# Two-layer routed FFN: the first stage's product into the ranks with the high and low halves of A in one weight

## The chip, the cores and the metric

The kernel runs on one core of one Trainium2 chip. The metric is the device time of one execution in microseconds. Before the change three runs took 981.65, 980.63 and 980.98 us: the median is 980.98 us.

## What is computed

Two layers work on x, 128 sequences of 32 tokens with 512 features (4096 tokens). Cut to the part that the change touches, with the rest in a line each:

```python
def _L0_cond_ref(x, adapter_mapping, W, b, lora_As, lora_Bs):   # W 512x512, As 32x512x16, Bs 32x16x512
    base_out = jnp.einsum('bti,oi->bto', x, W) + b
    A = lora_As[adapter_mapping]                # one adapter of 16 ranks for each sequence b
    Bm = lora_Bs[adapter_mapping]
    lora_h = jnp.einsum('bti,bir->btr', x, A)   # the product into the ranks
    lora_out = jnp.einsum('btr,bro->bto', lora_h, Bm)
    return base_out + lora_out * SCALING        # SCALING = 2

x = x + _L0_ffn_ref(_L0_cond_ref(x, itok_B_0_23, ...), ...)   # gate, up, silu, down; 1376 wide
x = x + _L1_ffn_ref(_L1_cond_ref(x, itok_B_0_7, ...), ...)    # routed, 8 experts of 16 ranks each
```

## The kernel before, in words

Features lie on the 128 partitions in KC = 4 chunks, tokens on the free axis, in NT = 8 tiles of TOK = 512 tokens. Float32 products are made of fp32r parts: ScalarE writes a rounded high part (`..._hi`), VectorE the rest (`..._lo`), and `mm3` (in `pe_program`) issues three matmuls, high weight x high, high weight x low and low weight x high. The low x low product is left out.

The work has three stages in order. The first makes c = `_L0_cond_ref(x)` of all tiles, in the first 142 us of the span. The second is the FFN of layer 0 in the form of a Strassen-like scheme over four pairs of tiles, up to about 805 us. The third folds layer 1's weights together and applies them with its routers. Only the first stage is changed; the others come after it on TensorE.

In the first stage a tile of 512 tokens holds 16 sequences, which form NG = 2 groups of GB = 8. The adapters of the 8 sequences of a group, 16 ranks each, make 128 columns. SyncE (for group 1 of tile 0: GpSimd) gathers them by `gather_a` into `a_raw`, one DMA a sequence; GpSimd gathers the rows of B into `b_raw`. `turn_a` in `act_program` (L1049) splits them into `a_hi` and `b_hi`, and its namesake in `dve_program` (L1510) makes `a_lo` and `b_lo`. `lora_in` in `pe_program` (L1978) is **the product into the ranks**: for each group and chunk, `mm3` with the 128 rank columns of all 8 sequences as the weight and the group's 256 tokens streaming. Each token thus gets the ranks of 8 sequences, of which only its own is wanted. `lora_in` in `dve_program` (L1521) masks the bank with `own_batch`, which is 1 where partition and token belong to the same sequence, and scales it by 2 into `h_masked`. ScalarE's `lora_in` (L1066) makes `lh_hi` of it, VectorE then `lh_lo`, and `lora_out` on TensorE (L2214) multiplies by B into the four banks of c. `close_c` on ScalarE (L1072) moves these to `c_out`, and GpSimd stores them to HBM. The weight that a matmul uses is loaded by an instruction of its own ahead of it (PEld in the profile).

The order on TensorE is written out by hand at the end of `pe_program`. Tiles 0 and 1 share their base product: after three of four chunks comes `lora_in(0)`, then the rest of the base, `lora_out(0)`, `lora_in(1)`, one more block of base matmuls (12 of 512 columns), `lora_out(1)`. From tile 2 on a tile is two base blocks of 12 (`cond_base`), `lora_in(t)`, two more blocks, `lora_out(t)`. ScalarE does for each tile `turn_a(t)`, the split of x for the next tile, `lora_in(t)`, then `close_c` mixed with splits of later weights (`down_hi`); VectorE the same on its side. From tile 6 on both also prepare the second stage: `cop_split` and `cop_begin`, `cop_rest` read the first c back from HBM (`load_c` on SyncE), and in tile 7 `gate_up_hi` and `gate_up_lo` split seven weights ahead of `lora_in`.

Semaphores tie the parts together: `a_lo_done` lets TensorE start a group, `pe_ring` says that the bank of ranks is full, `dve_freed` that VectorE has read it, `lh_lo_done` that `lora_out` may start.

Of the kernel before, what the change touches and what calls it, by code (L numbers as in the profile page):

```python
# [6 lines left out]
ALU = mybir.AluOpType  # L7
# [21 lines left out]
def build(nc, x, slots, slot_list, langs, w0, b0, a_cols, b_rows, w_gate, w_up, w_down, wb1, rhs2, ra1, b2t, b1, out):  # L29
# [65 lines left out]
    a_hi = work("a_hi", [NG, KC, P], F32R)  # L95
    a_lo = work("a_lo", [NG, KC, P], F32R)
# [37 lines left out]
    warm = work("warm", [TOK], F32R)  # L134

# [190 lines left out]
    a_hi_done, a_lo_done = sem("a_hi_done"), sem("a_lo_done")  # L326
    b_hi_done, b_lo_done = sem("b_hi_done"), sem("b_lo_done")
# [64 lines left out]
    ZEROS, ROWS = 1, 4  # L392
# [131 lines left out]
    def a_views(g, half):  # L524
        return (half[:, g, :, :].rearrange("p k (b r) -> p k b r", b=GB),
                a_raw[:, g, :, :].rearrange("p b (k r) -> p k b r", k=KC))
# [51 lines left out]
    def sync_program(e):  # L578
# [11 lines left out]
        def gather_a(t, gs=range(NG)):  # L590

            for g in gs:
                if t > 0:
                    e.wait_ge(a_lo_done, NG * (t - 1) + g + 1)
                for b in range(GB):
                    slot = e.snap(slot_regs[g * GB + b], min_val=0, max_val=a_cols.shape[0] - 1)  # L596
                    e.dma_start(a_raw[:, g, b, :], a_cols[bass.ds(slot, 1)].rearrange("s p c -> (s p) c")).then_inc(  # L597
                        a_in[g], DMA)
# [253 lines left out]
    def pool_program(e):  # L852
# [107 lines left out]
        for b in range(GB):  # L960
            slot = e.snap(slot_regs[b], min_val=0, max_val=a_cols.shape[0] - 1)
            e.dma_start(a_raw[:, 1, b, :], a_cols[bass.ds(slot, 1)].rearrange("s p c -> (s p) c")).then_inc(a_first_in, DMA)
# [74 lines left out]
    def act_program(e):  # L1037
# [11 lines left out]
        def turn_a(t):  # L1049
            for g in range(NG):  # L1050
# [7 lines left out]
                a_to, a_from = a_views(g, a_hi)  # L1058
                e.activation(a_to, a_from, ACT.Copy).then_inc(a_hi_done, 1)
            for g in range(NG):  # L1060
# [3 lines left out]
                e.activation(b_hi[t % 2][:, g, :], b_raw[g][:, :], ACT.Copy).then_inc(b_hi_done, 1)  # L1064

        def lora_in(t):  # L1066
            e.wait_ge(dve_freed, ring_freed("h", t, 0)[1])
# [424 lines left out]
    def dve_program(e):  # L1492
# [17 lines left out]
        def turn_a(t):  # L1510
            for g in range(NG):
                e.wait_ge(a_hi_done, NG * t + g + 1)
                a_to, a_from = a_views(g, a_lo)
                a_high, _ = a_views(g, a_hi)
                e.tensor_tensor(a_to, a_from, plain(a_high), ALU.subtract).then_inc(a_lo_done, 1)
            for g in range(NG):
                e.wait_ge(b_hi_done, NG * t + g + 1)
# [3 lines left out]
        def lora_in(t):  # L1521
# [4 lines left out]
            else:  # L1526
                e.wait_ge(lh_lo_done, t)
            e.scalar_tensor_tensor(
                out=h_masked[:, :].rearrange("p (g c) -> p g c", g=NG),
                in0=ring_bank("h", t, 0)[:, :].rearrange("p (g c) -> p g c", g=NG), scalar=SCALING,  # L1530
# [251 lines left out]
        assert links[0] == ZEROS  # L1782
        e.wait_ge(pool_const, 1)
# [591 lines left out]
```

## Time and profile before

| | |
|---|---|
| median of 3 runs | 980.98 us (980.63 to 981.65) |
| profiled execution, its own time | 981.22 us |
| its span, first to last instruction | 979.5 us |
| TensorE matmuls, busy | 972.1 us, 4723 |
| weight loads (PEld), busy | 822.1 us, 4723 |
| VectorE, ScalarE, GpSimd busy | 586.0, 464.5, 276.9 us |
| mean granted TensorE clock | 1.000 |

Times in the rows are in microseconds unless marked ns; ACT is ScalarE, DVE VectorE, POOL GpSimd, SP SyncE, PE TensorE. A row of a timeline holds the start, the time from the first start to the last end of the instructions merged in it, the engine, the line in the code, the operation, out<-in with its shape, and how many (x). In brackets stands how long the engine idled before, and what released it. Matmuls overlap, so the distance of two starts is less than the duration that a row shows.

### The profile page before, as it was taken

Reading aid. Unit: us, or ns where it says so; the run is one execution under the profiler, and the core shown is the slowest. Engines: PE = TensorE matmul, PEld = TensorE weight load, DVE = VectorE, ACT = ScalarE, POOL = GpSimd, SP = SyncE. Lnnn points to the kernel's source line nnn. Section 1 sums busy time; section 2 is a strip of 40 time slices with the busy share of each in tenths; the row PEclk is TensorE's granted clock in tenths of the full one; section 3 lists DMA queues with packets and bytes.
Section 4 is the critical chain, followed back from the end, with each engine's and each line's share of the span. In section 5 each row is a group of like instructions: output and inputs, shape, how many; then the busy total and the mean of one; then the engine's idle time right before and its main releaser. Section 6 shows DMA issues by size and latency. Waiting matters only on the chain.

```text
span 979.5 us, 14271 instructions
## 1 busy us (share of the span) xinstructions
PE 972.1 (99%) x4723; PEld 822.1 (84%) x4723; DVE 586.0 (60%) x970; ACT 464.5 (47%) x855; POOL 276.9 (28%) x284
## 2 busy tenths in 40 slices
PE   9999999999999999999999999999999999999998
PEld 7888888888888888888888888888888899898986
DVE  4545487876992432685423398333278488786862
ACT  4646476655742333571333383233357264545342
POOL 5363524654300721400522230261140460000000
PEclk9999999999999999999999999999999999999999
DMA  7899868686968866877886777987688650616132
GB/s 239 269 362 321 265 232 300 243 295 243 369 237 296 295 195 193 278 235 263 278 278 195 234 246 249 322 280 194 194 275 314 236 194 22 236 37 223 65 108 86
DMA packets 131123, 230.14 MB, mean 235 GB/s; under 512 B 29798, under 2 KB 29799, under 8 KB 130539
## 3 DMA queue, kind: packets, MB, share of 16 engines
q1 hardware_dynamic: 126720, 216.35, 66.4%
q0 software_dynamic: 4192, 12.87, 3.6%
q8 instruction: 39, 0.64, 0.3%
q14 instruction: 34, 0.27, 0.1%
q10 hardware_dynamic: 138, 0.01, 0.0%
HBM read 165.74 MB, written 63.44 MB: 234 GB/s over the span
## 4 chain that ended last, share of the span: by engine, by line
PE 87%; SPq 5%; DVE 2%; DMA 2%; issue 2%; ACT 1%; ACTq 0%; DVEq 0%
PE bank L1951 87%; SPq L597 3%; DMA x_raw<-in_x 1%; PE bank L2114 1%; SPq L583 1%; DMA c<-c_scratch 1%; SPq L588 0%; DMA a_raw<-in_a_cols 0%; SPq L664 0%; DVE xa_lo L1502 0%; ACT c_out L1076 0%; SPq L596 0%; ACT dt L1102 0%; SPq L772 0%; DVE hg L1762 0%
## 5 line engine op out<-in xcount | busy, mean ns | idle before, releaser
L1951 PE MATMUL bank<-cop_hi,wring 128*128 128x512 f32 x1234 | 380.9, 389 | 0.0
L1951 PEld LDWEIGHTS bank<-cop_hi,wring 128*128 128x128 f32 x1234 | 231.6, 188 | 48.8 <-DVE v L1590 0.4
L1951 PE MATMUL bank<-cop_lo,wring 128*128 128x512 f32 x616 | 239.7, 389 | 0.0
L1951 PE MATMUL bank<-op_hi,wring 128*128 128x512 f32 x560 | 173.8, 389 | 0.0
L1590 DVE TENSOR_TENSOR v<-bank,p7s 128x512 f32<-128x512 f32 x44 | 30.4, 691 | 194.0 <-PE bank L1951 193.9
L1951 PEld LDWEIGHTS bank<-cop_lo,wring 128*128 128x128 f32 x616 | 115.6, 188 | 24.0
L1951 PEld LDWEIGHTS bank<-op_hi,wring 128*128 128x128 f32 x560 | 105.1, 188 | 22.0 <-DMA wring<-wd_scratch 0.2
L1951 PE MATMUL bank<-op_lo,wring 128*128 128x512 f32 x280 | 108.9, 389 | 0.0
L1176 ACT ACTIVATE s<-bank 128x512 f32<-128x512 f32 x44 | 26.3, 597 | 112.6 <-PE bank L1951 112.6
L1576 DVE TENSOR_TENSOR op_lo<-h,op_hi 128x512 fp32r<-128x512 f32 x100 | 72.6, 743 | 3.7 <-ACT op_hi L1133 3.6
L909 POOL TENSOR_TENSOR h_t<-h,h 128x512 f32<-128x512 f32 x20 | 27.1, 1356 | 160.8 <-DVE h L1612 160.8
L1133 ACT ACTIVATE op_hi<-h 128x512 fp32r<-128x512 f32 x100 | 62.6, 626 | 13.9 <-PE bank L1951 12.8
L1145 ACT ACTIVATE bank<-bank 128x512 f32<-128x512 f32 x44 | 25.6, 583 | 76.5 <-PE bank L1951 76.5
L1951 PEld LDWEIGHTS bank<-op_lo,wring 128*128 128x128 f32 x280 | 52.6, 188 | 10.9
L948 POOL TENSOR_TENSOR t_sum<-x_second,x_second 128x256 f32<-128x256 f32 x12 | 9.4, 817 | 177.6 <-DMA x_second<-x_scratch 177.6
L1951 PE MATMUL bank<-xa_hi,w_hi 128*128 128x512 f32 x128 | 46.9, 392 | 1.2 <-ACT w_hi L1047 0.8
L1951 PE MATMUL bank<-xa_lo,w_hi 128*128 128x512 f32 x128 | 46.7, 390 | 0.0
L1951 PE MATMUL bank<-xa_hi,w_lo 128*128 128x512 f32 x128 | 46.5, 389 | 0.0
L1595 DVE TENSOR_TENSOR p7s<-bank,p7s 128x512 f32<-128x512 f32 x44 | 30.4, 691 | 24.9 <-PE bank L1951 24.9
L1167 ACT ACTIVATE s<-bank 128x512 f32<-128x512 f32 x44 | 26.3, 598 | 30.6 <-PE bank L1951 30.6
L1152 ACT ACTIVATE p7s<-bank 128x512 f32<-128x512 f32 x44 | 26.3, 598 | 30.2 <-PE bank L1951 30.1
L1160 ACT ACTIVATE bank<-bank 128x512 f32<-128x512 f32 x44 | 25.6, 582 | 30.0 <-PE bank L1951 30.0
(243 smaller groups left out, 1925.8 us busy)
## 6 DMA issues: line engine op xcount, KB each, us to landing
wring<-wgu_scratch SPq DMA_DIRECT2D x231, 256.0 KB, 3.1
wring<-wd_scratch SPq DMA_DIRECT2D x140, 256.0 KB, 5.5
wgu_scratch<-wring SPq DMA_DIRECT2D x77, 256.0 KB, 3.5
c_scratch<-c_out POOLq DMA_DIRECT2D x32, 256.0 KB, 3.3
c<-c_scratch SPq DMA_DIRECT2D x32, 256.0 KB, 4.7
xs_raw<-x_scratch SPq DMA_DIRECT2D x16, 512.0 KB, 5.2
out<-res SPq DMA_DIRECT2D x32, 256.0 KB, 2.1
x_raw<-in_x SPq DMA_DIRECT2D x14, 512.0 KB, 5.8
```

What stands on the lines that cost most here:

```text
L597: e.dma_start(a_raw[:, g, b, :], a_cols[bass.ds(slot, 1)].rearrange("s p c -> (s p) c")).then_inc(a_in[g], DMA)
L909: e.tensor_tensor(h_t3[p][:, :], h22[p][:, :], h12[p][:, :], ALU.subtract).then_inc(t3_done, 1)
L1133: e.activation(op_hi[n % N_OP][:, :], op_source[i][p][:, :], ACT.Copy).then_inc(op_hi_done, 1)
L1145: e.activation(bank_y[b][:, :], bank_a[b][:, :], ACT.Copy).then_inc(ay_done, 1)
L1152: e.activation(p7s[b][:, :], bank_w[b][:, :], ACT.Copy).then_inc(p7s_done, 1)
L1160: e.activation(bank_z[b][:, :], bank_y[b][:, :], ACT.Copy).then_inc(yz_done, 1)
L1167: e.activation(s1[j % 2][:, :], bank_a[j % 2][:, :], ACT.Silu).then_inc(silu1_done, 1)
L1176: e.activation(s2[j % 2][:, :], bank_z[j % 2][:, :], ACT.Silu).then_inc(silu2_done, 1)
L1576: e.tensor_tensor(op_lo[n % N_OP][:, :], op_source[i][p][:, :], plain(op_hi[n % N_OP][:, :]), ALU.subtract).then_inc(op_lo_done, 1)
L1590: e.tensor_tensor(v[b][:, :], bank_z[b][:, :], p7s[b][:, :], ALU.add).then_inc(gc22_done, 1)
L1595: e.tensor_tensor(p7s[b][:, :], bank_y[b][:, :], p7s[b][:, :], ALU.add).then_inc(gc21_done, 1)
L1951: return e.matmul(out_ap, lhs, rhs, start=start, stop=stop, skip_group_check=True)
```

## The change

In place of `a_hi` and `a_lo` there is one tile `a_both` with 256 columns for each group and chunk: low parts of four sequences (64 columns), high parts of all eight (128), low parts of the other four (64). Columns 0 to 127 are low and high of one half of the sequences, columns 128 to 255 high and low of the other half. `gather_a` puts the sequences into `a_raw` in the order that this takes (`a_place`). TensorE goes over each group twice, 128 tokens at a time, with the weight of the four sequences to which these tokens belong, and streams the high and the low part of x past it: two matmuls a chunk in place of three. The bank then holds the product with the high columns in one half of the partitions and with the low columns in the other; of the low ones also the part from the low x, which the kernel before left out. To add the halves, ScalarE copies each to the other half of the partitions (`lora_turn`, two operations, into `h_turned`), VectorE adds bank and `h_turned` into `h_masked`, and masks and scales that as before. VectorE makes the low columns in two operations a group. `h_turned` is cleared once at the start, so that its unused quarters are finite. The semaphores `a_hi_done` and `b_hi_done` become one.

```diff
--- before.py
+++ after.py
@@ -92,8 +92,7 @@
     within(h_region + 4 * ROW, h10_region - h_region - 4 * ROW)
     a_raw = work("a_raw", [NG, GB, KC * R], F32)
     b_raw = [work(f"b_raw{g}", [D], F32) for g in range(NG)]
-    a_hi = work("a_hi", [NG, KC, P], F32R)
-    a_lo = work("a_lo", [NG, KC, P], F32R)
+    a_both = work("a_both", [NG, KC, 2 * P], F32R)
     w0_hi = work("w0_hi", [KC, D], F32R)
     w0_lo = work("w0_lo", [KC, D], F32R)
     b_hi = [work(f"b_hi{s}", [NG, D], F32R) for s in range(2)]
@@ -132,6 +131,7 @@
 
     within(w_region, N_W * ROW)
     warm = work("warm", [TOK], F32R)
+    h_turned = sb("h_turned", [NG, GT], F32, w_region + 8 * ROW)
 
     gs_first = [sb(f"gs_first{i}", [2, P], F32, w_region + (N_W - 2) * ROW + (i - 1) * ROW // 2) for i in range(1, 5)]
 
@@ -323,8 +323,8 @@
     x_hi, x_lo = sem("x_hi"), sem("x_lo")
     l_hi, l_lo = sem("l_hi"), sem("l_lo")
     w0_hi_done, w0_lo_done = sem("w0_hi_done"), sem("w0_lo_done")
-    a_hi_done, a_lo_done = sem("a_hi_done"), sem("a_lo_done")
-    b_hi_done, b_lo_done = sem("b_hi_done"), sem("b_lo_done")
+    ab_hi_done, a_lo_done, b_lo_done = sem("ab_hi_done"), sem("a_lo_done"), sem("b_lo_done")
+    h_turned_done = sem("h_turned_done")
     lh_hi_done, lh_lo_done = sem("lh_hi_done"), sem("lh_lo_done")
     c_closed, l_closed = sem("c_closed"), sem("l_closed")
     act_freed, dve_freed = sem("act_freed"), sem("dve_freed")
@@ -389,7 +389,7 @@
 
     IDENT, MASK, LATER, EXPERT = 3, 6, 8, 9
 
-    ZEROS, ROWS = 1, 4
+    ZEROS, ROWS = 1, 5
 
     def x_parts(t):
 
@@ -521,9 +521,22 @@
 
 
 
-    def a_views(g, half):
-        return (half[:, g, :, :].rearrange("p k (b r) -> p k b r", b=GB),
-                a_raw[:, g, :, :].rearrange("p b (k r) -> p k b r", k=KC))
+    HB, HR = GB // 2, P // 2
+
+    def a_views(g, b, at_col):
+        n = b.stop - b.start
+        return (a_both[:, g, :, at_col:at_col + n * R].rearrange("p k (b r) -> p k b r", b=n),
+                a_raw[:, g, b, :].rearrange("p b (k r) -> p k b r", k=KC))
+
+    def a_place(b):
+
+        return (b + HB) % GB
+
+    def h_turns():
+
+        for rows, other, tok in ((slice(0, HR), slice(HR, P), slice(0, GT // 2)),
+                                 (slice(HR, P), slice(0, HR), slice(GT // 2, GT))):
+            yield rows, other, tok
 
     def g_sums(j):
         return gs_first if j == 0 else gs[j % 2]
@@ -594,7 +607,7 @@
                     e.wait_ge(a_lo_done, NG * (t - 1) + g + 1)
                 for b in range(GB):
                     slot = e.snap(slot_regs[g * GB + b], min_val=0, max_val=a_cols.shape[0] - 1)
-                    e.dma_start(a_raw[:, g, b, :], a_cols[bass.ds(slot, 1)].rearrange("s p c -> (s p) c")).then_inc(
+                    e.dma_start(a_raw[:, g, a_place(b), :], a_cols[bass.ds(slot, 1)].rearrange("s p c -> (s p) c")).then_inc(
                         a_in[g], DMA)
 
         def load_gate_up(j):
@@ -959,7 +972,7 @@
         e.reg_load(slot_regs, slot_sb[0:1, GB:2 * GB])
         for b in range(GB):
             slot = e.snap(slot_regs[b], min_val=0, max_val=a_cols.shape[0] - 1)
-            e.dma_start(a_raw[:, 1, b, :], a_cols[bass.ds(slot, 1)].rearrange("s p c -> (s p) c")).then_inc(a_first_in, DMA)
+            e.dma_start(a_raw[:, 1, a_place(b), :], a_cols[bass.ds(slot, 1)].rearrange("s p c -> (s p) c")).then_inc(a_first_in, DMA)
         gather(0)
         e.memset(own_batch[:, :], 1.0).then_inc(pool_const, 1)
         mask_view = own_batch[:, :].rearrange("p (b t) -> p b t", b=GB)
@@ -1055,15 +1068,27 @@
                     e.wait_ge(a_in[g], GB * DMA * (t + 1 - g))
                 if t > 0:
                     e.wait_ge(pe_ring, ring_full("h", t - 1, 0))
-                a_to, a_from = a_views(g, a_hi)
-                e.activation(a_to, a_from, ACT.Copy).then_inc(a_hi_done, 1)
+                a_to, a_from = a_views(g, slice(0, GB), HR)
+                e.activation(a_to, a_from, ACT.Copy).then_inc(ab_hi_done, 1)
             for g in range(NG):
                 e.wait_ge(b_in, NG * DMA * (t + 1))
                 if t > 1:
                     e.wait_ge(pe_acc, nth(t - 2))
-                e.activation(b_hi[t % 2][:, g, :], b_raw[g][:, :], ACT.Copy).then_inc(b_hi_done, 1)
+                e.activation(b_hi[t % 2][:, g, :], b_raw[g][:, :], ACT.Copy).then_inc(ab_hi_done, 1)
+
+        def lora_turn(t):
+            both = ring_bank("h", t, 0)[:, :].rearrange("p (g c) -> p g c", g=NG)
+            e.wait_ge(pe_ring, ring_full("h", t, 0))
+            if t == 0:
+                e.wait_ge(dve_chain, ZEROS + 1)
+            else:
+                e.wait_ge(dve_freed, ring_freed("h", t - 1, 0)[1])
+            for rows, other, tok in h_turns():
+                done = e.activation(h_turned[rows, :, tok], both[other, :, tok], ACT.Copy)
+            done.then_inc(h_turned_done, 1)
 
         def lora_in(t):
+            lora_turn(t)
             e.wait_ge(dve_freed, ring_freed("h", t, 0)[1])
             if t > 1:
                 e.wait_ge(pe_acc, nth(t - 2))
@@ -1509,12 +1534,14 @@
 
         def turn_a(t):
             for g in range(NG):
-                e.wait_ge(a_hi_done, NG * t + g + 1)
-                a_to, a_from = a_views(g, a_lo)
-                a_high, _ = a_views(g, a_hi)
-                e.tensor_tensor(a_to, a_from, plain(a_high), ALU.subtract).then_inc(a_lo_done, 1)
+                e.wait_ge(ab_hi_done, 2 * NG * t + g + 1)
+                for b, at_col, hi_col in ((slice(0, HB), 0, HR), (slice(HB, GB), P + HR, P)):
+                    a_to, a_from = a_views(g, b, at_col)
+                    a_high, _ = a_views(g, b, hi_col)
+                    done = e.tensor_tensor(a_to, a_from, plain(a_high), ALU.subtract)
+                done.then_inc(a_lo_done, 1)
             for g in range(NG):
-                e.wait_ge(b_hi_done, NG * t + g + 1)
+                e.wait_ge(ab_hi_done, 2 * NG * t + NG + g + 1)
                 e.tensor_tensor(b_lo[t % 2][:, g, :], b_raw[g][:, :], plain(b_hi[t % 2][:, g, :]),
                                 ALU.subtract).then_inc(b_lo_done, 1)
 
@@ -1525,9 +1552,13 @@
                 e.wait_ge(w0_lo_done, KC)
             else:
                 e.wait_ge(lh_lo_done, t)
+            both = ring_bank("h", t, 0)[:, :].rearrange("p (g c) -> p g c", g=NG)
+            whole = h_masked[:, :].rearrange("p (g c) -> p g c", g=NG)
+            e.wait_ge(h_turned_done, t + 1)
+            linked(e.tensor_tensor(whole, both, h_turned[:, :, :], ALU.add))
+            e.wait_ge(dve_chain, links[0])
             e.scalar_tensor_tensor(
-                out=h_masked[:, :].rearrange("p (g c) -> p g c", g=NG),
-                in0=ring_bank("h", t, 0)[:, :].rearrange("p (g c) -> p g c", g=NG), scalar=SCALING,
+                out=whole, in0=whole, scalar=SCALING,
                 in1=own_batch[:, :].unsqueeze(1).to_broadcast([P, NG, GT]),
                 op0=ALU.mult, op1=ALU.mult).then_inc(dve_freed, 1)
             e.wait_ge(lh_hi_done, t + 1)
@@ -1780,6 +1811,7 @@
 
         linked(e.memset(plain(warm[:, :]), 0.0))
         assert links[0] == ZEROS
+        linked(e.memset(h_turned[:, :, :], 0.0))
         e.wait_ge(pool_const, 1)
         linked(e.tensor_single_scalar(r_i[:, :], part_i[:, :], R - 1, ALU.bitwise_and))
         e.wait_ge(dve_chain, links[0])
@@ -1980,12 +2012,15 @@
             bank = take_h(t)
             for g in range(NG):
                 e.wait_ge(a_lo_done, NG * t + g + 1)
-                for k in range(KC):
-                    if g == 0:
-                        e.wait_ge(x_lo, x_n(t, k))
-                    tok = slice(g * GT, (g + 1) * GT)
-                    done = mm3(bank[:, tok], a_hi[:, g, k, :], a_lo[:, g, k, :],
-                               xa_hi[s][:, k, tok], xa_lo[s][:, k, tok], k == 0, k == KC - 1)
+                for first in (P, 0):
+                    at_tok = g * GT + (0 if first == P else GT // 2)
+                    tok = slice(at_tok, at_tok + GT // 2)
+                    for k in range(KC):
+                        if (g, first) == (0, P):
+                            e.wait_ge(x_lo, x_n(t, k))
+                        both = a_both[:, g, k, first:first + P]
+                        mm(bank[:, tok], both, xa_hi[s][:, k, tok], k == 0, False)
+                        done = mm(bank[:, tok], both, xa_lo[s][:, k, tok], False, k == KC - 1)
             done.then_inc(pe_ring, 1)
 
         def cond_base(t, m, k):
```

The order of instructions on TensorE, in the first tile's product into the ranks (`xa` is x, the number behind a name its buffer, x3 and x4 how many like it follow one another). Before:

```order
L1951 MATMUL bank<-xa_lo_72,w_hi 128x512 x3
L1951 MATMUL bank<-xa_hi_70,w_lo 128x512 x3
L1951 MATMUL bank<-xa_hi_69,a_hi 128x256
L1951 MATMUL bank<-xa_lo_71,a_hi 128x256
L1951 MATMUL bank<-xa_hi_69,a_lo 128x256
```

and with the change:

```order
L1983 MATMUL bank<-xa_lo_71,w_hi 128x512 x3
L1983 MATMUL bank<-xa_hi_69,w_lo 128x512 x3
L1983 MATMUL bank<-xa_hi_68,a_both 128x128
L1983 MATMUL bank<-xa_lo_70,a_both 128x128
L1983 MATMUL bank<-xa_hi_68,a_both 128x128
```

The three rows of 256 columns come eight times before, the two of 128 columns sixteen times with the change; what stands ahead and behind is unmoved.

The order on ScalarE in tile 2, before:

```order
L1064 ACTIVATE b_hi_61<-b_raw_55 128x512
L1064 ACTIVATE b_hi_61<-b_raw_56 128x512
L1043 ACTIVATE xa_hi_70<-x_raw_75 128x512 x4
L1070 ACTIVATE lh_hi_65<-h_masked 128x512
L1076 ACTIVATE c_out_51<-bank,b_287 128x512
```

and with the change:

```order
L1077 ACTIVATE b_hi_60<-b_raw_55 128x512
L1077 ACTIVATE b_hi_60<-b_raw_56 128x512
L1056 ACTIVATE xa_hi_69<-x_raw_74 128x512 x4
L1087 ACTIVATE h_turned<-bank 64x2x128 x2
L1095 ACTIVATE lh_hi_64<-h_masked 128x512
L1101 ACTIVATE c_out_51<-bank,b_287 128x512
```

The two copies stand between the split of x and `lh_hi`. On VectorE one addition stands ahead of the mask.

## Rows read from the trace of the kernel before

**Rows 1.** The page: TensorE's busy time, its granted clock in 40 slices, the chain

```profile
PE 972.1 (99%) x4723; PEld 822.1 (84%) x4723; DVE 586.0 (60%) x970; ACT 464.5 (47%) x855; POOL 276.9 (28%) x284
...
PEclk9999999999999999999999999999999999999999
...
PE 87%; SPq 5%; DVE 2%; DMA 2%; issue 2%; ACT 1%; ACTq 0%; DVEq 0%
```

**Rows 2.** Waits from 0 to 140 us: total, times, longest

```profile
PE bank L1951 <- DVE lh_lo L1534: 0.9, 1, 0.9
...
PE bank L1951 <- ACT c_out L1076: 0.4, 1, 0.4
```

**Rows 3.** Timeline of TensorE, first tile's product into the ranks and what follows

```profile
20.52 0.28 PE L1951 MATMUL bank<-xa_hi,a_hi 128*128 128x256 f32 x1
...
23.39 1.09 PE L1951 MATMUL bank<-xa_hi,w_hi 128*128 128x512 f32 x4
```

**Rows 4.** Timeline of loads (PEld), then of matmuls, behind tile 1's wait

```profile
37.73 0.19 PEld L1951 LDWEIGHTS bank<-lh_hi,b_hi 128*128 128x128 f32 x1 [1.32 <-DVE lh_lo L1534]
37.84 0.19 PEld L1951 LDWEIGHTS bank<-lh_lo,b_hi 128*128 128x128 f32 x1
37.96 0.19 PEld L1951 LDWEIGHTS bank<-lh_hi,b_lo 128*128 128x128 f32 x1
...
37.74 0.39 PE L1951 MATMUL bank<-lh_hi,b_hi 128*128 128x256 f32 x1 [0.90 <-DVE lh_lo L1534]
37.96 0.28 PE L1951 MATMUL bank<-lh_lo,b_hi 128*128 128x256 f32 x1
```

**Rows 5.** Timeline of TensorE's shortest matmuls, then of the loads behind them

```profile
846.50 1.09 PE L1951 MATMUL bank<-ra,hg1t 128*128 128x136 f32 x8
847.43 0.60 PE L2114 MATMUL bank<-ident,hg 128*128 128x128 f32 x4
...
847.75 0.19 PEld L1951 LDWEIGHTS bank<-hg_hi,m_hi 128*128 128x128 f32 x1
847.87 0.19 PEld L1951 LDWEIGHTS bank<-hg_lo,m_hi 128*128 128x128 f32 x1
```

**Rows 6.** 256 elements on ScalarE and VectorE (timelines); the page on a 512 add

```profile
129.18 0.72 ACT L1089 ACTIVATE wring<-gs_first 128x256 fp32r<-128x256 f32 x2
...
130.49 0.75 DVE L1540 TENSOR_TENSOR wring<-gs_first,wring 128x256 fp32r<-128x256 f32 x2
...
L1590 DVE TENSOR_TENSOR v<-bank,p7s 128x512 f32<-128x512 f32 x44 | 30.4, 691 | 194.0 <-PE bank L1951 193.9
```

**Rows 7.** Timelines of TensorE and VectorE in tile 3, from the product's end

```profile
65.73 0.40 PE L1951 MATMUL bank<-xa_hi,w_hi 128*128 128x512 f32 x1
...
71.20 0.28 PE L1951 MATMUL bank<-lh_hi,b_hi 128*128 128x256 f32 x1
...
66.63 0.68 DVE L1528 SCALAR_TENSOR_TENSOR h_masked<-bank,own_batch 128x512 f32<-128x512 f32 x1
68.01 0.84 DVE L1534 TENSOR_TENSOR lh_lo<-h_masked,lh_hi 128x512 fp32r<-128x512 f32 x1 [0.70 <-ACT lh_hi L1070]
```

**Rows 8.** Timelines of TensorE and VectorE in tile 1, from the product's end

```profile
33.81 0.28 PE L1951 MATMUL bank<-xa_hi,a_lo 128*128 128x256 f32 x1
33.93 0.40 PE L1951 MATMUL bank<-xa_hi,w_hi 128*128 128x512 f32 x1
...
35.62 0.67 DVE L1528 SCALAR_TENSOR_TENSOR h_masked<-bank,own_batch 128x512 f32<-128x512 f32 x1
36.99 0.69 DVE L1534 TENSOR_TENSOR lh_lo<-h_masked,lh_hi 128x512 fp32r<-128x512 f32 x1 [0.70 <-ACT lh_hi L1070]
```

**Rows 9.** Timelines of TensorE and ScalarE between tiles 6 and 7

```profile
123.99 0.28 PE L1951 MATMUL bank<-lh_hi,b_lo 128*128 128x256 f32 x1
124.71 0.50 PE L1951 MATMUL bank<-xa_hi,w_hi 128*128 128x512 f32 x1 [0.43 <-ACT c_out L1076]
...
120.50 0.63 ACT L1115 ACTIVATE cop_hi<-c 128x512 fp32r<-128x512 f32 x1 [0.20 <-DMA c<-c_scratch]
```

**Rows 10.** Timeline of VectorE in tile 7

```profile
135.18 0.69 DVE L1554 TENSOR_TENSOR c_t<-c,c 128x512 f32<-128x512 f32 x1 [2.60 <-DMA c<-c_scratch]
...
137.89 0.69 DVE L1534 TENSOR_TENSOR lh_lo<-h_masked,lh_hi 128x512 fp32r<-128x512 f32 x1 [0.70 <-ACT lh_hi L1070]
```

## The prediction

> **What bounds the kernel now.** I read the page first: TensorE is busy 99% of the span and holds 87% of the chain that ended last [rows 1]. So I took the waits of the first 140 us, where the changed stage lies: TensorE idles 0.9 us for `lh_lo` and 0.4 us for `c_out`, and nothing else there holds it up [rows 2]. The time is therefore the sum of what TensorE issues, one start after the other. A matmul's duration says little, since they overlap; what counts is the distance between starts, and that I take from TensorE's timeline.
>
> In the first tile's product into the ranks, 24 matmuls of 256 columns fill 20.52 to 23.39, where the next work starts: 2.87 us, 0.120 each [rows 3]. 24 matmuls of 512 columns fill 65.73 to 71.20: 0.228 each [rows 7]. The difference of 0.108 us is 256 columns at 2.4 GHz, the level that a granted clock of 1.00 is. So a matmul of n columns costs n/2.4 ns and some 13 ns, as long as its columns are what it waits for.
>
> **The change, part by part.**
>
> *Streamed columns.* A tile's product goes from 24 matmuls of 256 columns to 32 of 128, from 6144 to 4096 columns. By columns alone one of 128 would cost 53 + 13 = 67 ns and a tile 32 x 0.067 = 2.14 us in place of 2.87.
>
> *Weight loads.* But each matmul has its own load of 128 x 128 weights: as many of the one as of the other [rows 1, 3]. What a load costs when nothing covers it is seen after a wait: TensorE starts one at 37.73 and the next at 37.84. The matmul that is noted at 37.74 has 0.39 us where its like have 0.28, so it really ran 0.11 us later, when its load was through [rows 4]. In a stream, each load starts with the matmul ahead of it (both at 37.96): one load is under way per matmul, not two. So two starts cannot be closer than one load, about 0.108 us with 0.003 for the hand-over. The shortest distances in the trace agree: 8 matmuls of 136 columns fill 846.50 to 847.43, 0.116 us each, and 4 transposes of 128 columns last 0.60 us with 0.27 for the last, 0.11 us each [rows 5]. Both are plain fp32 and might be slow for another reason. But the loads at 847.75 and 847.87 are again a whole load apart, and the first is of the kernel's own kind. Under 256 columns (107 ns) a load was covered; under 128 it isn't. Bounds for the unseen case: 67 ns, and 0.111 + 0.013 = 0.124 us if the 13 ns come on top of the load. I take 0.111 us, which these measured loads are nearest to [rows 4, 5]: 32 x 0.111 = 3.55 us, **0.68 us more a tile, 5.4 us for eight**.
>
> The Trainium skill ("TensorE: Matmul & The Clock Gate", Back-to-back issue gap) has a measured sustained rate of about 81 ns for a load and a matmul of 128 columns. By that a tile would take 2.59 us and eight would save 2.2 us. The trace has no distance that short.
>
> *The way back to TensorE.* ScalarE now first turns two quarters of the bank: two operations of 256 elements, and a pair of these took 0.72 us [rows 6]. VectorE then adds (0.69, as an add out of a bank [rows 6]) before the old mask. From the mask's start to TensorE's next use it was 35.62 to 37.74, 2.12 us, the last hand-over in it 0.06 (37.68 to 37.74) [rows 4, 8]. With three more such hand-overs: 0.06 + 0.72 + 0.06 + 0.69 + 0.06 + 2.12 = 3.7 us from the product's end, 1.5 us more than before. The cover in tiles 2 to 7 is the 24 base matmuls behind the product, 5.5 us. In tile 3, the tightest of 2 to 6, `lh_lo` ended at 68.86, 2.3 us early [rows 7]. There the mask began at 66.63, 0.7 us behind the product's end, since VectorE was busy; the turning covers that. Left over: 5.5 + 0.1 - 0.3 - 3.7 = 1.6 us (a last matmul runs some 0.3 us past its start, and the next starts 0.1 behind it). So it costs nothing; without the cover it would be 1.5 us a tile. Tile 0 has 21 base matmuls, 4.8 us, and 0.9 us left.
>
> *Tile 1* has only 12, from 33.93 [rows 8]. They ended at 36.67, and TensorE waited until 37.74. The mask began 1.5 us behind the product's end, VectorE being held by tile 2's x, whose arrival does not hang on TensorE. Two longer products put TensorE 1.4 us later, which takes this part away, and the wait is again 0.3 + 3.7 - 2.85 = 1.1 us. Before: 1.1. Nothing; at worst 1.5 us, if x moves along with TensorE.
>
> *Tile 6 to 7.* At 124.71 TensorE starts 0.6 us late: ScalarE came late to `c_out`, since it had to split loaded c first, which came by DMA as late as 120.50 [rows 9]. TensorE will be 7 x 0.68 = 4.8 us later by then; the DMA less, since it hangs on earlier tiles. I count -0.6 us, with 0 for the bound.
>
> *Tile 7.* The mask was late here, behind sums of c that waited 2.60 us for DMA, and `lh_lo` ended at 138.58, just at its use [rows 10]. The turning is over by then; the add costs 0.7 us if the DMA moves with TensorE in full. With TensorE 5.4 us later I expect slack instead: 0, bound +0.7.
>
> *Small ones.* The low part of A in two pieces of 256 costs VectorE 2 x 0.34 us (0.75 less the last 0.41 [rows 6]), some 0.1 more than one of 512; TensorE needs the second group 1.4 us behind the first. `h_turned` is cleared once at the start, while VectorE waits for x. ScalarE is held at the turn, but its next job, `c_out`, waits for TensorE anyway.
>
> **Sum.** 5.4 - 0.6 = +4.8 us on the profiled execution's 981.22 gives 986.0; the median shown is 0.24 lower, so **985.8 us**.
>
> **Rivals.**
> 1. *Loads are hidden, columns decide.* If a load could start ahead of the matmul before it, or two neighbours with the same weights shared one, a tile costs 2.14 us: 8 x -0.73 = -5.8, 975 us, faster. It decides from a distance under 0.090 us, where 32 matmuls cost what 24 did. For it: 16 of 32 weights are repeats. Against: the loads measured [rows 4, 5], among them `b_hi` loaded twice in a row. 7%. By the 81 ns of the skill it is 978.8 us; 3%.
> 2. *The 13 ns come on top of the load.* 0.124 us, +1.10 a tile, 8.8 - 0.6, 989 us. In the range.
> 3. *The hand-over becomes a wait.* If ScalarE or VectorE comes to the turn so late that `lh_lo` misses its use by 1 us in each of tiles 2 to 6, +5 us on top, 991 us. For it: two more crossings between engines. Against: the 1.6 us left. 8%.
> 4. *The clock.* A stream that holds columns half of the time could let the granted clock fall to 1.2 GHz. It stayed 1.00 in every slice, waits and transposes included [rows 1]. If the 12 matmuls behind each product ran at that level, 0.43 us in place of 0.23, it would be +2.4 us a tile, 1005 us. 4%.
> 5. *The columns are not fewer.* The order of instructions shows 32 of 128 columns, so no.
>
> **Numbers.** A measurement of this kernel tells 0.2% (2 us) from no change. The forecast with its bounds has 74%; its range is 983.5 (0.102 us, a little under the shortest distance seen) to 990 (0.124 us, both small terms at their bad ends). A distance near 0.09 us, so no change, has 4%. With rival 3 the range to 991.5 holds 82%. Faster 10%, same 4%, slower 86%.
>
> **What would show it.** In the timeline after: loads and matmuls of the product 0.11 us apart; a product of 3.5 us; `lh_hi` some 1.4 us later behind it; no wait for `lh` in tiles 2 to 7, 1.1 us in tile 1, none near tile 6's `c_out`; the clock at 1.00; from 145 us on everything as before, only later. A product of 2.1 us would make me wrong in sign.

## The result and the profile after

The changed kernel took 986.75 us, the median of 4 runs (986.12 to 987.73), beside 981.32 us (980.63 to 982.16) for the kernel before: a ratio of 1.0054, 95% interval 1.0040 to 1.0068. Five more runs on another chip gave 985.95 beside 981.35 us, 1.0058 (1.0045 to 1.0071). The forecast was 985.8 us, range 983.5 to 991.5. The profiled execution took 986.12 us, with a span of 984.5 us; before it was 979.5.

The page of the changed kernel, the lines that answer to [rows 1]:

```profile
PE 978.0 (99%) x4787; PEld 828.4 (84%) x4787; DVE 592.2 (60%) x995; ACT 470.3 (48%) x871; POOL 282.1 (29%) x284
...
PEclk9999999999999999999999999999999999999999
...
PE 97%; DVE 2%; ACT 1%; DMA 0%; issue 0%; DVEq 0%; ACTq 0%
```

There are 64 matmuls more (8 tiles, 32 in place of 24), the clock is at its higher level throughout, and TensorE holds still more of the chain. What TensorE waited for from 0 to 145 us (total, times, longest), as in [rows 2]:

```profile
PE bank L1983 <- DVE warm L1812: 1.7, 1, 1.7
PE bank L1983 <- DVE lh_lo L1565: 1.0, 1, 1.0
```

The wait for `c_out` is gone; `warm` is from the start-up, before the changed stage's first product. The first tile's product in TensorE's timeline, which answers to [rows 3], and below it the loads:

```profile
20.85 0.22 PE L1983 MATMUL bank<-xa_hi,a_both 128*128 128x128 f32 x1
20.91 0.28 PE L1983 MATMUL bank<-xa_lo,a_both 128*128 128x128 f32 x1
21.02 0.27 PE L1983 MATMUL bank<-xa_hi,a_both 128*128 128x128 f32 x1
...
24.37 1.16 PE L1983 MATMUL bank<-xa_hi,w_hi 128*128 128x512 f32 x4
...
20.96 0.19 PEld L1983 LDWEIGHTS bank<-xa_hi,a_both 128*128 128x128 f32 x1
21.07 0.19 PEld L1983 LDWEIGHTS bank<-xa_lo,a_both 128*128 128x128 f32 x1
```

Matmuls and loads alike start 0.11 us apart, and 32 matmuls fill 20.85 to 24.37: 3.52 us, where 24 took 2.87. The first step is only 0.06 us, and that comes back when the stream ends: the second 512-column matmul behind the product starts 0.29 us after the first, where before it was 0.24. From the product's first matmul to that second one it is 3.81 us in all eight tiles, and 3.11 before: **+0.70 us a tile, 5.6 us in all**.

The way back in tile 3 (ScalarE, VectorE, TensorE), which answers to [rows 7]:

```profile
69.18 0.77 ACT L1087 ACTIVATE h_turned<-bank 64x256 f32<-64x256 f32 x2 [2.49 <-PE bank L1983]
...
70.08 0.69 DVE L1558 TENSOR_TENSOR h_masked<-bank,h_turned 128x512 f32<-128x512 f32 x1 [1.87 <-ACT h_turned L1087]
...
70.81 1.47 DVE L1560 SCALAR_TENSOR_TENSOR h_masked<-h_masked,own_batch 128x512 f32<-128x512 f32 x1
...
72.98 1.00 DVE L1565 TENSOR_TENSOR lh_lo<-h_masked,lh_hi 128x512 fp32r<-128x512 f32 x1 [0.70 <-ACT lh_hi L1095]
...
74.53 0.28 PE L1983 MATMUL bank<-lh_hi,b_hi 128*128 128x256 f32 x1
```

The turning took 0.77 us (forecast 0.72) and the add 0.69, as forecast. The mask took 1.47 us here and `lh_lo` 1.00, where either took 0.69 in tiles 4 to 7 (in tile 2 it was 1.08 and 1.00); `lh_lo` still ended 0.55 us ahead of its use. That slack was 0.96 us in tile 0, 0.95 in tile 2, 1.64 in tiles 4 to 6 and 1.47 in tile 7. Tile 1, from the product's end (TensorE, ScalarE, VectorE), answers to [rows 8]:

```profile
35.64 0.44 PE L1983 MATMUL bank<-xa_hi,w_hi 128*128 128x512 f32 x1
...
39.61 0.39 PE L1983 MATMUL bank<-lh_hi,b_hi 128*128 128x256 f32 x1 [0.99 <-DVE lh_lo L1565]
...
35.84 0.77 ACT L1087 ACTIVATE h_turned<-bank 64x256 f32<-64x256 f32 x2 [0.67 <-PE bank L1983]
...
36.74 0.69 DVE L1558 TENSOR_TENSOR h_masked<-bank,h_turned 128x512 f32<-128x512 f32 x1 [0.74 <-ACT h_turned L1087]
...
38.86 0.69 DVE L1565 TENSOR_TENSOR lh_lo<-h_masked,lh_hi 128x512 fp32r<-128x512 f32 x1 [0.70 <-ACT lh_hi L1095]
```

Tiles 6 to 7 on TensorE [rows 9], then tile 7 on VectorE [rows 10] and TensorE's use of `lh_lo`:

```profile
129.52 0.28 PE L1983 MATMUL bank<-lh_hi,b_lo 128*128 128x256 f32 x1
129.64 0.40 PE L1983 MATMUL bank<-xa_hi,w_hi 128*128 128x512 f32 x1
...
138.58 0.69 DVE L1585 TENSOR_TENSOR c_t<-c,c 128x512 f32<-128x512 f32 x1 [1.42 <-DMA c<-c_scratch]
...
142.02 0.69 DVE L1565 TENSOR_TENSOR lh_lo<-h_masked,lh_hi 128x512 fp32r<-128x512 f32 x1 [0.70 <-ACT lh_hi L1095]
...
144.19 0.28 PE L1983 MATMUL bank<-lh_hi,b_hi 128*128 128x256 f32 x1
```

**The account.** The second stage starts at 147.06 us, 5.45 later than before (141.61). Tile 0's product began 0.33 us later, from the start-up. The products cost 5.6 us. In tile 1 the two starts around the wait are 1.375 us apart and were 1.288: +0.1. The late start in tile 7 (0.71 us where 0.12 is usual) is gone: -0.6. These make 5.4. Three starts of 0.34 to 0.39 us in place of 0.23 in the second stage's first 10 us (at 141.9, 150.2 and 150.5 before) are gone too, 0.4 us given back, and the span is 5.0 us longer.

### The profile page after: what moved, and what is told of

It reads as the page before. It is cut to its first block, busy times and chain, and to the rows that moved or that the text cites. A ratio compares the mean times of both kernels' runs of the same rounds, so it can differ in the third digit from the quotient of the medians.

```text
span 984.5 us, 14449 instructions
## 1 busy us (share of the span) xinstructions
PE 978.0 (99%) x4787; PEld 828.4 (84%) x4787; DVE 592.2 (60%) x995; ACT 470.3 (48%) x871; POOL 282.1 (29%) x284
## 4 chain that ended last, share of the span: by engine, by line
PE 97%; DVE 2%; ACT 1%; DMA 0%; issue 0%; DVEq 0%; ACTq 0%
PE bank L1983 96%; PE bank L2149 1%; DMA x_raw<-in_x 0%; DVE t_lo L1684 0%; DVE hg L1793 0%; DVE greater L1773 0%; ACT t_hi L1260 0%; DVE lx L1809 0%; DVE wins L1769 0%; DVE rank L1776 0%; DVE greater L1767 0%; ACT h_turned L1087 0%; DVE res L1701 0%; DVE h_masked L1560 0%; DVE lh_lo L1565 0%
```

## The experiments

**What sets the distance.** Three kernels change one size of the product's matmuls each, and keep 32 of them a tile. `half_columns` streams 64 tokens in each, so it leaves out the ranks of half of the tokens:

```diff
+                        tok_ = slice(at_tok, at_tok + GT // 4)
-                        mm(bank[:, tok], both, xa_hi[s][:, k, tok], k == 0, False)
+                        mm(bank[:, tok_], both, xa_hi[s][:, k, tok_], k == 0, False)
```

(and `xa_lo` alike).

> The changed kernel with each of the 32 matmuls of a tile's product into the ranks streaming 64 columns in place of 128, so half of the tokens get no ranks; the loads are as they were. If the distance of two starts is one weight load, nothing moves: 0.111 us each, a product of 3.5 us, 986.5 us or so. If it is set by the columns (128 / 2.4 ns and a fixed part of 58 ns), it falls to 0.084 us, 0.85 us less a tile, 980 us.

TensorE in the first tile's product:

```profile
20.87 0.28 PE L1983 MATMUL bank<-xa_hi,a_both 128*128 128x64 f32 x1
20.98 0.28 PE L1983 MATMUL bank<-xa_lo,a_both 128*128 128x64 f32 x1
```

Half the columns, and still 0.11 us: the columns don't set it. The profiled execution took 985.53 us with a span of 983.9. The median of 4 is 988.02 us, ratio 1.008 (1.0052 to 1.0107), because two executions took 990.5 and 992.7 us with a mean granted clock of 0.994 and 0.993; the other two took 985.5 us. Those with the lower clock were not profiled, so what brought it down stays open. `half_weights` keeps 128 tokens and loads 64 weight columns; it leaves out the half of the result that the other 64 give:

```diff
-                        both = a_both[:, g, k, first:first + P]
-                        mm(bank[:, tok], both, xa_hi[s][:, k, tok], k == 0, False)
+                        both = a_both[:, g, k, first:first + P // 2]
+                        mm(bank[0:P // 2, tok], both, xa_hi[s][:, k, tok], k == 0, False)
```

> The changed kernel with only the first 64 of the 128 weight columns in each matmul of the product (64 partitions of the bank get a result), all else the same, 128 tokens streaming. If the load sets the distance and costs by its columns, it falls to what 128 streamed columns need, 0.067 us: 32 x 0.044 = 1.4 us less a tile, 11.3 us in all, 975.5 us. If the load is a fixed time, or the distance is a floor for issuing a load and a matmul, it stays at 0.111 us and 986.5 us.

```profile
21.25 0.22 PE L1983 MATMUL bank<-xa_hi,a_both 128*64 128x128 f32 x1
21.31 0.22 PE L1983 MATMUL bank<-xa_lo,a_both 128*64 128x128 f32 x1
```

With the load halved the same 128 columns stream every 0.060 us. So the distance is not a fixed price for issuing a load and a matmul: **it is the load's**. `half_weights` also halves the partitions that a matmul writes, but the load's own record shrinks with it, from 0.192 to 0.135 us, by 0.057 us where the distance shrinks by 0.051. But the kernel took 982.04 us (10 runs, ratio 1.0000, 0.9987 to 1.0012) and not 12.9 us less than the change (8 x 1.61). In tile 1 TensorE now stood for `lh_lo`:

```profile
39.30 0.58 PE L1983 MATMUL bank<-lh_hi,b_hi 128*128 128x256 f32 x1 [3.35 <-DVE lh_lo L1565]
39.68 0.41 PE L1983 MATMUL bank<-lh_lo,b_hi 128*128 128x256 f32 x1
...
30.49 0.63 ACT L1072 ACTIVATE a_both<-a_raw 128x512 fp32r<-128x512 f32 x1 [3.07 <-DMA a_raw<-in_a_cols]
...
32.06 2.41 ACT L1101 ACTIVATE c_out<-bank,b 128x512 f32<-128x512 f32 x4
...
35.54 0.77 ACT L1087 ACTIVATE h_turned<-bank 64x256 f32<-64x256 f32 x2
```

The start distance there is 3.73 us in place of 1.38, since ScalarE's queue up to the turn (`b_hi`, `c_out`, `xa_hi`) hangs on the gather of A, for which ScalarE waited until 30.49 us. Behind this wait the clock fell: the matmul at 39.68 shows 0.41 us where its like have 0.28, its followers start 0.21 us apart, and the use of `lh` took 5.29 us in place of 2.97. Further waits stand at 99.3, 125.6 and 139.1 us (start distances of 0.62, 1.27 and 0.69): TensorE's saved time went into waits for other engines and into the lower clock. `wide_columns` streams all 256 tokens of the group in each of the 32, so half of the ranks are those of the wrong sequences:

```diff
+                    tok = slice(g * GT, (g + 1) * GT)
```

> The changed kernel with each of the 32 matmuls streaming all 256 tokens of its group, twice the columns; the second pass overwrites the first, so half of the ranks are those of the wrong sequences. Load theory: 256 columns just cover a load, so the distance is the 0.120 us seen before: +0.3 us a tile, +2.3 us in all, 989 us, though the columns double. Column theory (a fixed 58 ns on top of the columns): 0.165 us, +1.7 us a tile, 1000 us.

```profile
22.89 0.28 PE L1983 MATMUL bank<-xa_hi,a_both 128*128 128x256 f32 x1
23.00 0.28 PE L1983 MATMUL bank<-xa_lo,a_both 128*128 128x256 f32 x1
```

Twice the columns cost 0.26 us a tile (4.07 for 3.81). The time was 988.26 us (4 runs, ratio 1.0065, 1.0050 to 1.0079); its profiled execution also began the first product 2 us late. In a table, with the median distance of two starts in the product (the last column takes 0.111 us for a load of 128 weight columns, and half of it for 64):

| weight columns x tokens | distance, us | by columns (n/2.4 + 13 ns) | by the load |
|---|---|---|---|
| 128 x 64 | 0.112 | 0.040 | 0.111 |
| 128 x 128 | 0.111 | 0.067 | 0.111 |
| 128 x 256 | 0.120 | 0.120 | 0.111 |
| 64 x 128 | 0.060 | 0.067 | 0.056 |

The larger of the two columns fits the three rows with a full weight. At 64 x 128 the two nearly meet, and the measured 60 ns lies between them, so the 13 ns are not a fixed price either.

**The two halves of the change, each alone.** `chain_alone` keeps the turning and the add but issues the product as before (with the wrong columns of A for the low part). `product_alone` is the reverse: 32 matmuls of 128 columns, without turning and add, so the low half of the product is left out. The matmuls of `chain_alone`:

```diff
+                    done = mm3(bank[:, tok], a_both[:, g, k, P // 2:P // 2 + P], a_both[:, g, k, 0:P],
+                               xa_hi[s][:, k, tok], xa_lo[s][:, k, tok], k == 0, k == KC - 1)
```

and, of `product_alone`, the lines without turning and add:

```diff
-            lora_turn(t)
-            linked(e.tensor_tensor(whole, both, h_turned[:, :, :], ALU.add))
-                out=whole, in0=whole, scalar=SCALING,
+                out=whole, in0=both, scalar=SCALING,
```

> The changed kernel with TensorE's product as before, 24 matmuls of 256 columns (the wrong columns of A for the low part, so the result is not the reference's); the turning by ScalarE, the extra add and the split low part of A stay. My theory: the way back is hidden, so this is the kernel before within 1 us (981 to 982 us), with the waits in tile 1 0.9 to 1.5 us longer than before at worst. Rival: the longer way back is what the change costs, then it shows most of the 5.4 us, 985 us or more.

> The changed kernel with its 32 matmuls of 128 columns but without the turning and the add: the mask reads the bank, and the low half of the product is lost. My theory: all of the cost stays but what tile 1's wait gives, 985 to 986.5 us. Rival (the way back costs): it falls to the kernel before, 981 us.

`chain_alone` took 983.13 us (12 runs) beside 981.47, 1.0015 (1.0007 to 1.0024). So the way back alone, without the longer product, costs 1.7 us, more than the 1 us expected. The profiled execution was the slowest of the twelve (984.9 us). Its tile 1 on TensorE, ScalarE's wait for the gather ahead of it, and one window (busy times, granted clock, DMA share, GB/s):

```profile
39.64 0.39 PE L1983 MATMUL bank<-lh_hi,b_hi 128*128 128x256 f32 x1 [2.48 <-DVE lh_lo L1565]
...
40.87 0.41 PE L1983 MATMUL bank<-lh_hi,b_hi 128*128 128x256 f32 x1
41.08 0.41 PE L1983 MATMUL bank<-lh_lo,b_hi 128*128 128x256 f32 x1
...
30.84 0.63 ACT L1072 ACTIVATE a_both<-a_raw 128x512 fp32r<-128x512 f32 x1 [3.27 <-DMA a_raw<-in_a_cols]
...
40.00:60.00 20.00, 20.00 (x114) 18.07 (x113) 10.45 (x18) 11.02 (x21) 12.87 (x11) 0.91 1.00 352
```

The two starts around the wait are 2.87 us apart, 1.58 more than in the trace of the kernel before, and 1 us behind it the clock fell. In tiles 3 and 7 `lh_lo` ended just at its use as well (start distances 0.46 and 0.37 us). But the longer chain is not all of the 1.58 us. The mask started 1.88 us later than before (37.50 for 35.62), and 1.00 of that is the gather of A, for which ScalarE waited until 30.84 us here and until 29.84 in the trace of the kernel before; 0.88 is the turning and the add, and TensorE itself came 0.32 us later. This gather moves without any change to the first tiles. In `before_order` below, where everything up to tile 6 is the kernel before (the rows of before, then those of `before_order`):

```profile
29.84 0.63 ACT L1059 ACTIVATE a_hi<-a_raw 128x512 fp32r<-128x512 f32 x1 [2.90 <-DMA a_raw<-in_a_cols]
...
31.16 0.63 ACT L1059 ACTIVATE a_hi<-a_raw 128x512 fp32r<-128x512 f32 x1 [3.22 <-DMA a_raw<-in_a_cols]
...
39.05 0.39 PE L1952 MATMUL bank<-lh_hi,b_hi 128*128 128x256 f32 x1 [1.88 <-DVE lh_lo L1534]
```

The mask starts 5.8 us behind `a_hi` in both, since `b_hi`, `c_out`, `xa_hi` and VectorE's `xa_lo` stand between. With the gather 1.3 us later the start distance is 2.27 us in place of 1.29, and the clock fell behind it. `before_light` (31.04 us, 2.32 us) shows the same. **So the one trace of the kernel before, on which the forecast rests, had one of the shorter waits in tile 1.** The changed kernel doesn't feel the gather there: in both its traces ScalarE stood waiting for the product when it came to the turn (0.67 us in the first), and the distance was 1.38 and 1.37 us.

`product_alone` took 984.84 us (6 runs), 1.0030 (1.0018 to 1.0042). To set it beside the whole change on one chip, both ran again:

> The changed kernel once more, beside its own part product_alone (32 matmuls of 128 columns, no turning and no add) and the kernel before. If the longer way from the product back to TensorE is covered, as forecast, this run equals product_again within 0.5 us and both stand some 5 us over the kernel before. The earlier runs, on separate chips, had 986.75 us here and 984.84 us for product_alone, against 981.3 and 981.5 us of the kernel before: so the rival says that 1 to 2 us of the change belong to the way back.

> As product_alone: leaves out the turning and the add, so each token lacks part of its ranks' sum. Way back covered: the same as after_again, 986 to 987 us. Way back not covered: 1 to 2 us under after_again, 985 us.

985.95 us (5 runs, 985.67 to 988.02) for the change, and 984.98 us (5 runs, 984.40 to 985.43; 1.0044, 1.0031 to 1.0057) without the way back: 1.0 us apart where at most 0.5 was expected, so in the changed kernel the way back is not free. In the second trace of `product_alone` the place is plain: the mask starts as soon as the product ends, and TensorE runs on into `lh_hi` (TensorE, then VectorE):

```profile
37.90 0.39 PE L1979 MATMUL bank<-xa_hi,w_lo 128*128 128x512 f32 x1
38.12 0.28 PE L1979 MATMUL bank<-lh_hi,b_hi 128*128 128x256 f32 x1
...
35.51 0.69 DVE L1556 SCALAR_TENSOR_TENSOR h_masked<-bank,own_batch 128x512 f32<-128x512 f32 x1
36.90 0.69 DVE L1561 TENSOR_TENSOR lh_lo<-h_masked,lh_hi 128x512 fp32r<-128x512 f32 x1 [0.70 <-ACT lh_hi L1094]
```

No wait in tile 1 here, with the gather of A in use at 29.58 us; in the first trace, where it was 31.29, the distance was 0.96 us from start to start.

**Can the halves in one weight be had without short matmuls?** `two_banks` joins the high and the low x of 128 tokens into one matmul of 256 columns, from tile 2 on: 16 matmuls a tile into two banks, and two adds more on VectorE. It computes what the changed kernel does.

```diff
+                            done = mm(h_banks(t)[g][:, q * GT:(q + 1) * GT].rearrange("p (n c) -> p n c", n=2),
+                                      a_both[:, g, k, first:first + P], xa_parts[:, :, s, k, tok],
+                                      k == 0, k == KC - 1)
...
+                    linked(e.tensor_tensor(to, part[:, :, 0, :], other, ALU.add))
+                    linked(e.tensor_tensor(to, part[:, :, 1, :], to, ALU.add))
```

> The same result with half of the loads: from tile 2 on a matmul streams the high and the low part of x of its 128 tokens, 256 columns in all, past one load, into separate columns of two banks; ScalarE turns a group's quarters while TensorE still works on the other group, and VectorE adds in two steps a group. Load theory: 16 x 0.120 = 1.92 us for a product in place of 3.52, six tiles: -9.6 us from the changed kernel, 977 us, 4 us under the kernel before. If the column count alone set the time, the 4096 columns are the same and it stays at 986.5 us. If the longer way through ScalarE and VectorE misses the next use in some tiles, up to 1 us each comes back.

A product took 2.15 us, 1.66 less than in the change and 0.96 less than before. Yet the time was 982.47 us (12 runs, 1.0007, 0.9999 to 1.0016). In tile 5 TensorE stood for the low part of A (TensorE, ScalarE, windows):

```profile
96.17 1.11 PE L2012 MATMUL bank<-xa_parts,a_both 128*128 128x256 f32 x8
99.36 1.22 PE L2012 MATMUL bank<-xa_parts,a_both 128*128 128x256 f32 x8 [2.08 <-DVE a_both L1559]
...
97.89 0.63 ACT L1078 ACTIVATE a_both<-a_raw 128x512 fp32r<-128x512 f32 x1 [4.64 <-DMA a_raw<-in_a_cols]
...
80.00:100.00 20.00, 17.92 (x103) 15.46 (x102) 11.16 (x23) 11.03 (x24) 4.92 (x6) 1.00 1.00 335
100.00:120.00 20.00, 20.00 (x103) 17.28 (x103) 13.06 (x26) 11.37 (x25) 13.15 (x16) 0.91 0.90 286
```

The gather landed late at a DMA share of 1.00, and the clock fell behind the wait. `lh_lo` was late too, in tile 2 (start distance 1.00 us, behind a mask of 2.41 us) and in tile 7 (1.63 us), so here the way back cost time as well. To stay out of the late gather, `mixed` leaves tiles 0 to 3 as before and takes the two banks from tile 4 on (`SPLIT = 4`). It also masks ahead of the first sums of c in tile 7, a move that `before_order` makes alone:

```diff
+            lora_in(t)
+            if t == NT - 1:
                 cop_begin(0, 1)
-            lora_in(t)
```

> The kernel before with one move on VectorE: in tile 7 the mask and the low part of the ranks' result stand ahead of the first sums of c, which wait 2.60 us for DMA. In the kernel before that low part ended 0.08 us behind its use, so TensorE lost next to nothing there. If tile 7 costs nothing: within 0.5 us of the kernel before. If the sums of c, now later, hold up the second stage's start: 0.5 to 1.5 us slower. It is the control for mixed, which has this move too.

> The product as in the kernel before in tiles 0 to 3, and in tiles 4 to 7 as in two_banks: 16 matmuls of 256 columns, the high and the low part of x in one matmul and two banks. No load is uncovered at 256 columns, and the late tiles leave the gather of A more time. From the lengths measured before, 2.15 us in place of 2.87 us of the kernel before in 4 tiles: -2.9 us, and the wait of 1 us in tile 1 stays as it is. Load theory, with all waits covered: 978.5 us. If the gather of A (DMA share 0.94 to 1.00 in this stretch) or the way back takes the gain again, as in two_banks: 980.5 to 982 us.

`before_order` took 980.86 us (12 runs, 0.9999, 0.9989 to 1.0009): no difference. `mixed` took 980.97 us (11 runs, 1.0001, 0.9992 to 1.0011), which undoes the change's loss but gains nothing. The wait in tile 5 had come back, and behind it one for `lh_lo` (start distance 1.01 us). TensorE, ScalarE, window:

```profile
99.04 1.22 PE L2013 MATMUL bank<-xa_parts,a_both 128*128 128x256 f32 x8 [2.31 <-DVE a_both L1562]
...
97.56 0.63 ACT L1079 ACTIVATE a_both<-a_raw 128x512 fp32r<-128x512 f32 x1 [4.87 <-DMA a_raw<-in_a_cols]
...
80.00:100.00 20.00, 17.69 (x104) 15.42 (x104) 10.93 (x21) 10.81 (x23) 5.04 (x7) 1.00 1.00 333
```

The last gather of that group was issued at 91.3 us, and ScalarE waited until 97.56 for it; in the kernel before it was issued at 91.8 and had landed at 94.9. The last pair asks whether the DMA's load does this. In both kernels SyncE's stores of W_down's sums, and their later reads, take 16 of 128 partitions, so most of the down product is left out:

```diff
+            few = P // 8
-            e.dma_start(wd_dram[g, i][:, 0:c, :],
+            e.dma_start(wd_dram[g, i][0:few, 0:c, :],
```

> before_order with less to move: of the sums of W_down that SyncE stores to scratch ahead of each gather of A (14 stores of 512 KB from 20 to 140 us), only 16 of 128 partitions are stored and later read back, so the output is without most of the down product. TensorE's instructions stay the same. This is the baseline of mixed_light. In before TensorE waits 0.9 us for the ranks of tile 1 and 0.4 us for c_out and nothing for the gather, so both theories expect before_order's time less at most 1.5 us: 979.5 to 981 us.

> mixed with the same lighter stores; the output is without most of the down product. mixed had four products of 2.15 us in place of 3.11 us, 3.8 us in all, but its time was the kernel before's: TensorE stood 2.6 us in tile 5 for the low part of A, whose last gather had landed shortly before, at a DMA share of 1.00, and 1.0 us for lh_lo. If the DMA's load took the gain: no wait at tile 5 here, and 3 to 4 us under before_light, some 976.5 us. If the gather's own chain (one small DMA after another, released by VectorE's low part) or the engines' order took it, whatever else is moved: the wait at tile 5 stays at 1 to 2.6 us and the time is within 1.5 us of before_light.

`before_light` took 981.08 us (11 runs, 0.9998, 0.9989 to 1.0007), `mixed_light` 977.51 us (8 runs, 0.9968, 0.9957 to 0.9978): 3.6 us less, where four products of 0.96 us less make 3.8. Tile 5 of `mixed_light` (TensorE, window):

```profile
95.59 2.08 PE L2015 MATMUL bank<-xa_parts,a_both 128*128 128x256 f32 x16
...
80.00:100.00 20.00, 20.00 (x116) 17.65 (x115) 14.80 (x29) 12.05 (x27) 9.40 (x8) 1.00 0.82 236
```

No wait, and a DMA share of 0.82. A shorter product is thus worth its full length, and what took it back was the DMA's load. The lightened stores stand ahead of the gathers of A on SyncE's queue, so the pair does not tell whether the gathers gained by less traffic or by less in front of them. The kernel before had a share of 0.96 in the same stretch, so it had little room.

## Why the prediction was right, point by point

- *What bounds.* TensorE's issue, start after start: right. 5.0 us of span are 5.6 of product and small terms.
- *Weight loads, 0.111 us each, 5.4 us.* Right: 0.110 measured as a mean, 5.6 us with what comes back at the stream's end. That a load isn't hidden behind another, read from [rows 4, 5], is what the table shows; that it starts together with the matmul ahead is not so here (20.96 for 20.91). Rival 1 falls with it: behind a product's first step no two starts with 128 x 128 weights were less than 0.108 us apart in the traces of the changed kernel. The Trainium skill ("TensorE: Matmul & The Clock Gate", Back-to-back issue gap) has about 81 ns for a load and a matmul of 128 columns; this case does not agree, with 111 ns for its fp32r operands. Rival 2 falls too: the 13 ns don't come on top of the load. (The forecast's upper end with both small terms at their worst adds up to 990.5 us, 8.8 and 0.7 on 980.98, and not to 990.)
- *The way back is hidden.* Right for tile 0 (0.96 us left for a forecast 0.9) and tiles 2 to 7, where nothing waited for `lh`. The slack in tiles 4 to 6 was 1.64 us for a forecast 1.6, but 0.95 and 0.55 in tiles 2 and 3: the mask, priced at 0.68 us, took 1.08 and 1.47 there. Rival 3 was nearer than the rows of one tile let it look.
- *Tile 1, 1.1 us of wait as before.* The size after is right (1.15 us), and so is the way there: the two longer products took the lateness away, and what is left is the chain's length less the cover. The forecast "nothing" is the net of two terms: with the longer product alone the wait is 0.7 us or none, with the longer way back alone it was 2.6, 1.0 of it by a later gather. So of the change's loss 1.0 us (985.95 less 984.98) belongs to the way back. The cause named is wrong in the kernel before already: VectorE was held not by x's arrival but by ScalarE's `xa_hi`, which stood behind `b_hi` and `c_out` and a wait for the gather of A until 29.84 us. And "before: 1.1" was luck in part: it is 1.1 in the one trace read, and 2.0 and 2.1 in those of `before_order` and `before_light`.
- *Tile 6 to 7, -0.6.* Right.
- *Tile 7, nothing.* Right: the sums of c waited 1.42 us for DMA and not 2.60, and `lh_lo` had 1.47 us to spare. `before_order` adds that the place costs nothing before either.
- *Sum.* The +4.8 was +5.0 in span, and +5.4 and +4.6 between the medians of the two pairs. Not forecast: 0.3 us of start-up, which differs from one execution to the next, and 0.4 us given back at the second stage's start.
- *The clock.* It stayed, as forecast. Not the short matmuls but waits brought it down in other kernels; only the two unprofiled executions of `half_columns` leave the former open.

## What to carry to other kernels

Fewer streamed columns gain nothing once a matmul streams for less time than its weights take to load: here 128 columns cost what 64 do, and 256 only 9 ns more. Count the loads first, then the columns, and join short streams that share a weight into one matmul. Before an engine's work is cut, ask what else has nearly no slack: here TensorE was busy for 99% of the span and the DMA share was 0.96 from 80 to 100 us, and four shorter products were worth nothing until the DMA was relieved. And read a wait that ends with a DMA in more than one trace before it goes into a sum.

## What the runs showed of the hardware that was not expected

- **The clock behind a wait.** Six profiled executions had two TensorE starts over 2.2 us apart in the first stage behind the start-up: 2.27 and 2.32 (`before_order`, `before_light`), 2.36 (`two_banks`), 2.59 (`mixed`), 2.87 (`chain_alone`) and 3.73 us (`half_weights`). In five of them the matmuls behind ran at the lower level for a time (256 columns in 0.21 us, 512 in 0.43), within 2 us of the wait's end; `mixed` stayed at 1.00. Where the longest was 1.7 us or less, both profiled executions of the changed kernel included, it never fell. A lost microsecond can thus cost more than two: in `before_order` the wait in tile 1 is 1.0 us longer than in the trace of before, and tile 2's product starts 2.5 us later behind tile 1's. Of 82 executions of the kernel before, eight show a mean granted clock of 0.998; their median is 983.1 us, that of the others 981.3. The nine of the changed kernel show 0.999 or 1.000.
- **A halved load halves the distance.** 64 weight columns in place of 128 took a stream of 128-column matmuls from 0.111 to 0.060 us.
- **The same operation took 0.69, 1.08 or 1.47 us** on VectorE, the mask in tiles 4, 2 and 3 of one execution, and 2.41 in tile 2 of `two_banks`. Why was not tried.
